# A four-layer transformer on one core: two units per transposing DMA in the fourth attention, bias on VectorE, and the squared-relu feed-forward in f32 with its weights quantised ahead

## The reference, cut to what matters

```python
# third attention (L2_xattn): 32 heads of 8, keys and queries normalised
q = _rmsnorm(q); k = _rmsnorm(k)
attn = softmax(einsum('bhnd,bhmd->bhnm', q, k) * scale)
# third feed-forward (L2_ffn)
def _ternary_weight(w, group_size):            # groups of 64 along a row of w
    wb = w.astype(jnp.bfloat16); wg = wb.reshape(-1, group_size)
    scale = clip(mean(abs(wg), -1), 1e-08, None)
    return clip(round(wg / scale), -1, 1) * scale
h = square(relu(einsum('bsd,hd->bsh', x, _ternary_weight(W_fc, 64))))   # 1024 hidden
out = einsum('bsh,dh->bsd', _rms_norm(h), _ternary_weight(W_proj, 64))
# fourth attention (L3_xattn): 16 heads of 16, all 1024 tokens attend to all 1024
q = _fq_sym(q, axis=-1); k = _fq_sym(k, axis=-1); v = _fq_sym(v, axis=2)
attn = softmax(einsum('bhqd,bhkd->bhqk', q, k))
s = max(attn, -1) / 255; attn = clip(round(attn / s), 0, 255) * s
out = einsum('bhqk,bhkd->bhqd', attn, v)
```

## Time and profile before

| what | value |
|---|---|
| median of three runs | 1208.64 us (1208.03 to 1210.03) |
| the profiled execution, its own time | 1204.26 us |
| its span, first to last instruction | 1202.5 us |
| mean granted TensorE clock | 0.833 of full speed |
| busy: PE, DVE, ACT, POOL | 78%, 55%, 47%, 21% of the span |

### The profile page before, as it was taken

One profiled execution on the slowest core, in us unless ns is written; L12 is line 12 of the kernel. 1 busy time (PEld: TensorE's weight loads), 2 busy tenths in 40 slices (PEclk: granted clock), 3 DMA queues, 4 the chain that ended last, 5 costly groups with the idle time before them and its releaser, 6 DMA issues. The chain is left out here.

```text
span 1202.5 us, 16226 instructions
## 1 busy us (share of the span) xinstructions
PE 937.2 (78%) x5648; PEld 530.0 (44%) x5648; DVE 657.8 (55%) x1205; ACT 566.2 (47%) x844; POOL 249.0 (21%) x389
## 2 busy tenths in 40 slices
PE   5688888996983487994367637677777589999998
PEld 3244446663771344342136422222223456666665
DVE  4577735444357754225796737788889431111224
ACT  3166662222226655786263146788788222222211
POOL 3010100000000022001241105666667014000013
PEclk9599998997996799996598956655555679999999
DMA  3512201003110047621000756999999402111112
GB/s 127 131 32 74 80 16 35 1 1 115 66 52 1 1 147 169 145 73 44 0 1 1 282 173 142 188 186 175 180 180 186 116 32 88 35 44 45 31 38 89
DMA packets 179922, 105.85 MB, mean 88 GB/s; under 512 B 141253, under 2 KB 168079, under 8 KB 178063
## 3 DMA queue, kind: packets, MB, share of 16 engines
q1 hardware_dynamic: 174994, 97.61, 34.7%
q0 software_dynamic: 1536, 4.20, 1.1%
q10 hardware_dynamic: 3312, 3.02, 0.7%
HBM read 57.66 MB, written 16.38 MB: 62 GB/s over the span
## 5 line engine op out<-in xcount | busy, mean ns | idle before, releaser
L2272 ACT ACTIVATE sb_l_E<-PS,sb_l_NB,sb_L3SQS 128x1024 int16<-128x1024 f32 x128 | 154.0, 1203 | 42.6 <-POOL sb_l_NB L2231 40.5
L2281 DVE TENSOR_REDUCE sb_l_NM<-PS 128x1 f32<-128x1024 f32 x128 | 154.3, 1221 | 32.7 <-PE PS L2250 30.5
L2250 PE MATMUL PS<-sb_l_K,sb_l_Q 128*128 128x512 bf16 x256 | 123.6, 585 | 18.6 <-ACT sb_l_E L2272 17.0
L682 DVE TENSOR_REDUCE sb_negmax<-PS 128x2 f32<-128x512 f32 x128 | 84.1, 690 | 31.9 <-PE PS L532 31.7
L1387 ACT ACTIVATE sb_hidden<-PS 128x512 f32<-128x512 f32 x39 | 23.3, 598 | 164.2 <-PE PS L1341 164.2
L2222 POOL CAST sb_l_EB<-sb_l_E 128x1024 bf16<-128x1024 int16 x96 | 99.4, 1036 | 5.8
L2260 PEld LDWEIGHTS PS<-sb_L3VI,sb_l_ET 128*128 128x128 bf16 x1024 | 42.8, 107 | 130.9 <-DMA sb_l_ET<-sb_l_EB 121.6
L1422 DVE TENSOR_TENSOR sb_hidden<-sb_hidden,PS 128x512 f32<-128x512 f32 x39 | 26.8, 688 | 124.8 <-ACT sb_hidden L1387 124.8
L668 ACT ACTIVATE sb_E<-PS 128x1024 f32<-128x1024 f32 x64 | 65.5, 1023 | 42.5 <-PE PS L595 42.4
L1341 PE MATMUL PS<-sb_L3w,sb_block_xT 128*128 x184 | 82.8, 592 | 0.0
L2260 PE MATMUL PS<-sb_L3VI,sb_l_ET 128*128 128x16 bf16 x1024 | 49.6, 177 | 39.7 <-DMA sb_l_ET<-sb_l_EB 37.5
(11 more groups left out here) (355 smaller groups left out, 1821.8 us busy)
## 6 DMA issues: line engine op xcount, KB each, us to landing
sb_Q<-q SPq DMA_DIRECT2D x48, 192.0 KB
sb_L3w<-L3w SPq DMA_DIRECT2D x16, 512.0 KB, 8.9
sb_K<-k SPq DMA_DIRECT2D x24, 192.0 KB
sb_W2E<-L3w SPq DMA_DIRECT2D x8, 512.0 KB, 9.2
q<-sb_q_parts SPq DMA_DIRECT2D x12, 256.0 KB, 4.0
xs<-zero_row SPq DMA_DIRECT2D x1, 2944.0 KB, 47.3
sb_block_x<-xs SPq DMA_DIRECT2D x23, 128.0 KB, 2.2
ys<-sb_block_y ACTq DMA_DIRECT2D x23, 128.0 KB, 2.4
```

Source lines behind the costliest of these rows:

```text
L682: dve.tensor_reduce(NM[:, g, 2 * b:2 * b + 2, j:j + 1], core.bank(shared_bank(("max", m))).rearrange("p (u k) -> p u k", k=SEQ), axis=AX.X ...
L2250: ins = pe.matmul(core.bank(2 * (n % SRING) + half), Q[:, h % RING, t * P:(t + 1) * P], K[:, h % RING, half * HALF:(half + 1) * HALF], sta ...
L2272: act.activation(E[:, n % ERING, :], S(n), ACT.Exp, bias=NB[:, n:n + 1], scale=scale_of(h, t), accum_out=ZS[:, n:n + 1]).then_inc(exped, 1)
L2281: dve.tensor_reduce(NM[:, n:n + 1], S(n), axis=AX.X, op=ALU.max, negate=True).then_inc(maxed, 1)
```

## The change

Three things are changed.

1. **Fourth attention.** The exponential is rounded to one byte and written at every second byte, so that units 2m and 2m+1 interleave in one buffer of 1024 two-byte elements. One DMA transposes both (64 DMAs in place of 128) with no cast ahead of it. Behind it POOL casts each unit's bytes to bf16, all 128 of them, and PE mixes from that, eight units behind the scores in place of seven. The bias is made by DVE right behind its maximum, with a wait for it.
2. **Third feed-forward.** One block. PE multiplies in f32: two matmuls of 512 columns for a unit going up, eight of 256 columns for a tile going down. No splitting remains; ACT makes relu and second square, DVE the square, POOL the sum. Means, root and sums into X come in two halves of four tiles.
3. **Quantised weights.** They are loaded as they stand in DRAM, not transposed, and quantised within the steps of the third attention: POOL casts, DVE sums groups of 64 and compares, POOL subtracts and multiplies, a DMA transposes, POOL widens to f32 into the place where they were loaded. The work lies in the idle `q_parts` and `k_parts`.

```diff
@@ attention_l2
+                for i in range(2):                                    # SP, behind all loads
+                    sp.wait_ge(weighted, i + 1)
+                    sp.dma_start_transpose(QWT.rearrange("p (b n) -> p b n", n=P), QW).then_inc(w_turned, 16)
...
+                def cast_weights(i):                                  # POOL
...
+                    pool.tensor_copy(WB, ffn_weights[i].rearrange("p a b -> p (a b)")).then_inc(cast, 1)
+                def sign_weights(i):
+                    pool.wait_ge(below, 4 * (i + 1))
+                    pool.tensor_tensor(ABOVE, ABOVE, BELOW, ALU.subtract).then_inc(signed, 1)
...
                 for g in range(GROUPS):
+                    if g == 1:
+                        cast_weights(0)
+                    if g == 2:
+                        sign_weights(0)
+                        weight_signs(0)
+                        cast_weights(1)
+                    if g == 4:
+                        widen(0)
+                    if g == 5:
+                        sign_weights(1)
+                        weight_signs(1)
+                    if g == 7:
+                        widen(1)
...
                 for s in range(1, NS, 2):                             # DVE, one pair
+                    for i in range(2):
+                        for m in range(2 * (n - FIRST_PAIR[i]), 2 * (n - FIRST_PAIR[i]) + 2):
+                            if 0 <= m < 13:
+                                quantise_weights(i, m)
@@ ffn_relu2: the first block and the splits are gone
-                    for c in range(NC):
-                        for i in range(PARTS):
-                            ins = pe.matmul(core.bank(n % URING), Q1[:, c, k * P:(k + 1) * P],
-                                            XP[:, i, c, th * HALF:(th + 1) * HALF],
+                    for c in range(NC):
+                        ins = pe.matmul(core.bank(n % 2), up_weights[:, k, c, :],
+                                        core.XT[:, c, th * HALF:(th + 1) * HALF], start=(c == 0), stop=(c == NC - 1))
@@ attention_l3
-    PER, BRING, TRING, LAG = 1, 6, 8, 7
+    RING, SRING, ERING, TRING, CRING = 4, 3, 4, 5, 4
+    CAST_LAG, LAG = 6, 8
-    by_pool = [u % 8 in (0, 1, 2, 4, 5, 6) for u in range(NU)]
+    by_pool = [True for u in range(NU)]
+                for m in range(NU // 2):
+                    sp.wait_ge(exped, 2 * m + 2)
...
+                return eng.tensor_copy(ET[:, u % CRING], EP[:, u // 2 % TRING, :, :, u % 2])
...
+                    act.activation(E[:, n // 2 % ERING, :, n % 2], S(n), ACT.Exp, bias=NB[:, n:n + 1],
+                                   scale=scale_of(h, t), accum_out=ZS[:, n:n + 1]).then_inc(exped, 1)
...
+                        dve.wait_ge(maxed, n + 1)
+                        dve.tensor_scalar(NB[:, n:n + 1], NM[:, n:n + 1], scale_of(h, t), LN255,
+                                          ALU.mult, ALU.add).then_inc(biased, 1)
```

More of the change, by code:

```diff
@@ L746, in attention_l2 @@
     NS = len(steps)
+    GROUP, LIMIT, QUARTER, FIRST_PAIR = 64, 0.5 + 2.0 ** -9, 512, (7, 18)
+    cast, reduced, scaled_w, above, below, signed, weighted, w_turned = (core.sem(n) for n in (
+        "cast", "reduced", "scaled_w", "above", "below", "signed", "weighted", "w_turned"))
     names = ("q_projected", "v_projected", "squared", "meaned", "logged", "inverted", "scaled", "high", "rest", "middle",
@@ new lines, in ffn_relu2 @@
+    up_weights = W1.rearrange("p k (c n) -> p k c n", c=NC)
+    down_weights = W2.rearrange("p c (k n) -> p c k n", k=HC)
+    names = ("up", "relued", "squared", "quart", "pooled", "meaned", "eps_added", "rooted", "inverted", "down",
+             "one_made", "added")
+    (up, relued, squared, quart, pooled, meaned, eps_added, rooted, inverted, down,
+     one_made, added) = (core.sem(n) for n in names)
+    units = [(th, k) for th in range(2) for k in range(HC)]
+    NU = len(units)
+    down_bank = lambda t: core.PS[:, 3 + t // 2, (t % 2) * D:(t % 2 + 1) * D] if t < 4 else core.PS[
+        :, (2, 5, 6, 7)[t - 4], 0:D]
@@ L1941, in _, with mean @@
+                def mean(th):
+                    pe.wait_ge(pooled, HC * (th + 1))
+                    for j in range(4):
+                        ins = pe.matmul(core.PS[:, th, j:j + 1], SUM[:, th, j * P:(j + 1) * P], ONE[:, :],
+                                        start=True, stop=True)
+                    ins.then_inc(meaned, 1)
+                for n in range(HC + 2):
                     go_up(n)
-                pe.wait_ge(p3, HC)
+                pe.wait_ge(squared, HC)
                 for j in range(4):
@@ L1944, in _ @@
                     for k in range(HC):
-                        go_down(j, k)
-                    go_up(HC + 4 + j)
-                pe.wait_ge(relued, NU)
+                        ins = go_down(j, k)
+                    ins.then_inc(down, 1)
+                    go_up(HC + 2 + j)
+                for n in range(HC + 6, NU):
+                    go_up(n)
+                pe.wait_ge(relued, NU - 1)
+                pe.wait_ge(one_made, 1)
+                mean(0)
                 for k in range(HC):
-                    pe.wait_ge(p3, HC + k + 1)
+                    pe.wait_ge(squared, HC + k + 1)
@@ L1950, in _ @@
                     for t in range(4, 8):
                         ins = go_down(t, k)
[L1952 to L1958 removed]
+                        if k == HC - 1:
+                            ins.then_inc(down, 1)
@@ L1972, in _, with root @@
             def _(act):
-                for n in range(NU + 2):
+                def root(th):
+                    T = slice(4 * th, 4 * th + 4)
+                    act.wait_ge(eps_added, th + 1)
+                    act.activation(RS[:, T], MS[:, T], ACT.Sqrt).then_inc(rooted, 1)
+                for n in range(NU + 1):
                     if n < NU:
```

281 lines of the change are left out of this document (108 added, 173 removed).

## The result

The changed kernel takes 1148.19 us (median of 4 runs, 1146.27 to 1150.45) against 1208.99 us for the kernel before on the same chip: ratio 0.950, 95% interval 0.948 to 0.952. The forecast was 1159 us, with a range of 1147 to 1181. The profiled execution fell from 1204.26 to 1146.27 us, by 58.0; the forecast was 49.3.

A forecast was written before the change was run, and what follows sets the result against it. SP's queue of transposing DMAs was taken to bound the fourth attention, waiting chains the feed-forward. 1204.26 - 33.0 (feed-forward) + 1.4 (quantising) - 17.7 (fourth attention) = 1155.0; with 4.38 for the median, 1159 us, range 1147 to 1181.

The forecast's parts named there:

- the likeliest case: Whole kernel: feed-forward shortened, fourth attention freed from its DMA queue and paced by DVE; 1152 to 1165 us, chance 0.45.
- the offset: Whole kernel: the median of the runs lies 4.38 us above the profiled execution, so that much is added.
- Feed-forward, start at 559.95 + 57.0: Third feed-forward: PE starts at 559.95 and needs 57.0 us for f32 matmuls and means, one behind another.
- Port, 2.3 us: Third feed-forward: DVE's square and POOL's sum exclude each other, 2.1 us a unit against PE's 1.72; costs 2.3 us.
- Tail, 2.3: End of third feed-forward: DVE's four remaining tiles and root end 2.3 us behind PE's end.
- Quantising, +1.4: Third attention: quantising mostly hides; 1.1 us lost at pair 7, 0.3 behind the last widening, 1.4 us more (0 to 10).
- Fourth attention, DVE at 1.39 x 1.04: Fourth attention: DVE is next bound at 1.39 us a unit, 1.45 with 4% jitter; 16.0 us less over 127 steps.
- ACT at 1.36: Fourth attention: two exponentials on ACT stand 1.36 us apart where nothing holds the second.
- Rival A: Fourth attention: DVE's bias waits for POOL's casts, pace 1.55 or 1.65 us a unit, total 1172 or 1185; chance 0.30.
- B: Fourth attention: casts of bytes, or exponentials, take twice as long; casts give 2.07 us a unit, total 1240, slower; chance 0.05.
- C: Third attention: the quantising is not hidden and costs 10 us, total 1168; chance 0.08.
- D: No port loss in the feed-forward and a faster fourth attention at 1.40 us a unit, total 1150; chance 0.12.

The follow-up runs named there:

- E11: The changed kernel itself, unaltered, run again on another occasion; 1149.11 us, ratio 0.953 to the kernel before.
- E5: Changed kernel with no bias made in the fourth attention, ACT taking a constant and waiting for the maximum; ratio 0.932 to the kernel before.
- E4: Changed kernel with a further POOL copy of 256 elements ahead of each feed-forward sum; ratio 0.953 to the kernel before.
- E2: Kernel before with only the fourth attention changed, feed-forward and its weights as before; ratio 0.982 to the kernel before.
- E7: Changed kernel with a quarter of the fourth attention's casts on DVE, as before the change; ratio 0.973 to the kernel before.
- E8: Changed kernel with each transposing DMA of the fourth attention issued twice, the second into a spare buffer; ratio 0.971 to the kernel before.
- E3: Changed kernel without the quantising of weights in the third attention, feed-forward using weights as loaded; ratio 0.953 to the kernel before.
- E10: Changed kernel with even units' biases on POOL, casts six units behind, mixing ten behind, last cast on DVE; ratio 0.948 to the kernel before.
- E9: Changed kernel with even units' biases on POOL, casts four units behind, mixing eight behind, last cast on DVE; ratio 0.954 to the kernel before.
- E12: As the changed kernel with even biases on POOL, casts six behind, mixing ten behind, but rings of six; 1141.01 us, ratio 0.946 to before.

## Why the prediction was right, and where its steps were off

The mechanism of the likeliest case held: DMA queue, then DVE. Its number was less good. The profiled execution saved 8.7 us more than the 49.3 forecast, and the median of 1148 lies outside the 1152 to 1165 that the prediction gave to this case, 1 us above the lower end of its range. Beside the 8.7 us the offset went its way: the median lies 1.9 us above the profiled execution, where the prediction added 4.4. By steps:

- **Feed-forward, start at 559.95 + 57.0.** Right. PE's prices from the other stage fit: 58.75 us busy, 57.0 + 1.8 for the clock, which stood at 0.69 over the first 5.4 us. The forecast for it was 2.8, between 1 and 4.5; the loss varies, for E11 had 0.74 and E5 0.50 over its first 5.4 us.
- **Port, 2.3 us.** Wrong size; it is 0. I counted POOL's sum at 1.34 and both lengths in full, 2.1 a unit against 1.72. The sum takes 1.26; the 1.34 of the earlier trace rows had itself waited for a DVE instruction that ran until 631.81:

```profile
631.12 0.69 DVE L2011 TENSOR_TENSOR sb_h_rest<-sb_h,sb_hparts 128x512 f32<-128x512 f32 x1
```

And 0.23 of a pair overlaps without harm, so that 1.95 fit into PE's 1.72. E4 shows that the exclusion is real and that even 2.04 costs nothing here, since the ten units going up end before it reaches PE. The Trainium skill ("SBUF — State Buffer", Who interferes with whom) says a DVE instruction with two SBUF inputs contends with a POOL instruction that reads SBUF; the squares of 1.34 and 1.66 us agree, but the lengths in a trace are not the time that the port is held.
- **Tail, 2.3.** It was 2.1. Together the stage saved 36.4 in place of 33.0; over all twelve profiles with the new block and the two without, 73.4 to 76.0 us pass from the last copy of the third attention to the last sum into X, against 109.3 and 110.0.
- **Quantising, +1.4.** Right in size (1.3 to 1.6) and in both places: 0.69 for pair 7 against 1.1 forecast, and 0.66 behind the last widening against 0.3. The first two profiles show a gain of 1.3 instead. PE waited 5.7 us less for the queries in the second of them, by chance: 2.9 to 11.9 us over fourteen profiles, 11.9 in the profile of before that I read. That fits steps that are 1.4 us shorter, but by E2 a shorter wait alone does not bring the feed-forward forward, so the cause of this 1.3 is not shown. A single pair of profiles misled here.
- **Fourth attention, DVE at 1.39 x 1.04.** The engine was right (E5, E7), the queue behind it too (E8), and the two errors in the number went against each other. Maximum and bias take 1.38 and not 1.33 (the bias lasts 0.214, where the earlier trace rows had 0.154 for one with a single operation and a constant), and 1.43 with the heads. The 4% of jitter was seen with the DMA queue as the bound; with DVE as the bound there is none. 18.7 in place of 16.0.
- **ACT at 1.36.** Wrong, and harmless only as DVE was above it. E5 has 1.18. It would have misjudged a next step that frees DVE: E5 gained 25 us in the maxima, where this number allows 127 x (1.428 - 1.36) = 8.6.
- **Rival A, 0.30.** It had too much weight. The row it rested on the earlier trace rows was of an operation with 1024 elements; DVE's biases, with one element, never waited (212 to 216 ns, 128 times). For casts it was right: 0.866 on average in E7.
- **Rivals B, C, D.** Cast and exponential at 1.04 and 1.21 refute B, and E3 refutes C's 10 us. D, at 0.12, came nearest in number: a median of 1150 against 1148, and a saving in the profile of 58.0 against 58.0. It had the feed-forward right (no port loss), but its pace of 1.40 was too fast (1.428), which with the end is 2.9 us too much saved; 2.7 at the start and 1.1 in the feed-forward make up for that, by luck.

## What to carry to other kernels

Name the engine that is late next, and then the one behind that, but take an engine's shortest spacing from a stretch where nothing can hold it: two instructions without a bracket of idle time may still have waited. A factor for jitter goes with the bound it was measured on. When one engine in a loop is full, look for a gap on another that recurs in step with it, and put the moved instruction where the waits ahead of it have long been met (E10 against E9).

## What the hardware did that I had not expected

- The granted clock in the fourth attention was 0.82 in E5, at 1.23 us a unit, and 0.56 in after at 1.43: 119.8 us of matmul for the same work in place of 142.2. The pace alone does not tell it, for E10 and E12, both at 1.36, had 0.63 and 0.53.
- An exponential with a sum does not wait for the read of the one ahead: the read at 761.49 lasts 0.23, and the next starts at 761.58.
- A bias on DVE, one element a partition with two operations and a pointer as one scalar, lasts 0.214 us, where the one of the earlier trace rows, with one operation and a constant, lasts 0.154; which of the two differences costs the 0.06 no run here separates. On POOL the bias lasts 0.265.
- DVE and POOL, which exclude each other for 0.7 us and more, still overlap at the edges by 0.10 to 0.13 us without a trace of it in either length.
